# Graph attention over edges: accumulation moved to TensorE and ScalarE

## The reference

```python
q, k, v = x @ Wq + bq, x @ Wk + bk, x @ Wv + bv      # by node, 8 heads
logits = einsum('ehd,ehd->eh', q[dst], k[src]) / sqrt(D)
seg_max = segment_max(logits, dst)
expv = exp(logits - seg_max[dst])
denom = segment_sum(expv, dst)
agg = segment_sum(expv / denom[dst] * v[src], dst)
out = agg + x @ Wskip + bskip                        # then gelu, residual, layer norm
```

## Time and profile before

| | us |
|---|---|
| median of 3 runs | 4432.44 (4432.07 to 4436.84) |
| the profiled execution | 4432.26, its span 4430.5 |
| VectorE busy | 3621.0 (82%) |
| TensorE busy: matmul, weight load | 3266.7 (74%), 2350.0 (53%) |
| GpSimd busy | 2724.9 (62%) |
| ScalarE busy | 2404.3 (54%) |

### The profile page before, as it was taken

One profiled execution on the slowest core, in us unless ns is written; L12 is line 12 of the kernel. 1 busy time (PEld: TensorE's weight loads), 2 busy tenths in 40 slices (PEclk: granted clock), 3 DMA queues, 4 the chain that ended last, 5 costly groups with the idle time before them and its releaser, 6 DMA issues. The chain is left out here.

```text
span 4430.5 us, 103464 instructions
## 1 busy us (share of the span) xinstructions
PE 3266.7 (74%) x25228; PEld 2350.0 (53%) x25229; DVE 3621.0 (82%) x10151; ACT 2404.3 (54%) x5817; POOL 2724.9 (62%) x2719
## 2 busy tenths in 40 slices
PE   7886877877787877878787877347888888887620
PEld 3335666666666666666666666244555555555410
DVE  8888989989898988989898989876666676676457
ACT  4435666666566656666665666454555555555310
POOL 3226766667666766667676665117777777777750
PEclk9988999999999999999999999558999999999855
DMA  6537767667677766777676766521121121111147
GB/s 221 176 124 222 220 207 212 206 208 218 206 212 207 221 203 204 212 208 219 195 221 206 221 200 185 194 95 22 30 34 31 30 34 31 31 30 30 26 83 279
DMA packets 367713, 677.14 MB, mean 153 GB/s; under 512 B 70294, under 2 KB 240482, under 8 KB 367074
## 3 DMA queue, kind: packets, MB, share of 16 engines
q0 software_dynamic: 157888, 420.64, 35.7%
q1 hardware_dynamic: 97474, 128.43, 8.3%
q10 hardware_dynamic: 111712, 120.75, 8.1%
HBM read 582.00 MB, written 87.58 MB: 151 GB/s over the span
## 5 line engine op out<-in xcount | busy, mean ns | idle before, releaser
L736 POOL DMA_INDIRECT KV<-kv_d,src_i x1564 | 1609.1, 1029 | 798.6 <-issue 438.1
L1370 POOL DMA_INDIRECT re_src<-src_tab_d,rsrc x1024 | 985.0, 962 | 311.9 <-issue 245.2
L997 PE MATMUL agg_ps<-msg,oh 128*128 128x264 f32 x3512 | 872.2, 392 | 12.7 <-DVE msg L827 12.7
L997 PEld LDWEIGHTS agg_ps<-msg,oh 128*128 128x128 f32 x3512 | 639.3, 192 | 130.2 <-issue 34.1
L956 PE MATMUL Q<-q,ohT 128*128 128x256 bf16 x5328 | 672.7, 277 | 1.7 <-issue 0.5
L827 DVE TENSOR_TENSOR msg<-KV,msg 128x1024 f32<-128x1024 f32 x439 | 538.4, 1226 | 154.9 <-issue 107.8
L885 ACT ACTIVATE off<-dst_f,wbase 128x4 f32 x447 | 132.9, 297 | 854.7 <-issue 806.6
L893 ACT ACTIVATE square<-iota_b,off 128x128 bf16<-128x128 bf16 x1784 | 568.1, 389 | 0.3
L835 DVE TENSOR_TENSOR prod<-KV,Q 128x1024 f32<-128x1024 f32 x443 | 538.0, 1214 | 3.3 <-issue 1.3
L839 DVE TENSOR_REDUCE lg<-prod 128x32 f32<-128x1024 f32 x443 | 535.5, 1209 | 0.2
L956 PEld LDWEIGHTS Q<-q,ohT 128*128 128x128 bf16 x5328 | 496.3, 99 | 64.1 <-issue 2.2
(11 more groups left out here) (259 smaller groups left out, 5618.6 us busy)
## 6 DMA issues: line engine op xcount, KB each, us to landing
q<-q_d ACTq DMA_DIRECT2D x446, 192.0 KB
y_d<-ex_y ACTq DMA_DIRECT2D x56, 448.0 KB
rg_ye<-y_d SPq DMA_DIRECT2D x7, 3584.0 KB, 12.0
KV<-kv_d,src_i POOLq DMA_INDIRECT x1564
nu_xs<-xs_d SPq DMA_DIRECT2D x7, 2688.0 KB, 11.8
re_src<-src_tab_d,rsrc POOLq DMA_INDIRECT x1024
kv_d<-pr_kv SPq DMA_DIRECT2D x49, 256.0 KB, 2.2
xs_d<-pr_xs SPq DMA_DIRECT2D x49, 256.0 KB, 2.3
```

Source lines behind the costliest of these rows:

```text
L736: pool.indirect_dma_start(out=KV[:, t % (KVR * G), :], out_offset=None, in_=k.kv_d, in_offset=bass.IndirectOffsetOnAxis(ap=k.src_i[:, t:t ...
L997: m = pe.matmul(agg_ps[:, 0:HEADS * HW], oh32[ring(s, 2)][:, t, :], msg[ring(s, 2)][:, t, :, :].rearrange("p h e -> p (h e)"), start=(t == ...
L1370: pool.indirect_dma_start(out=gs[:, t % (RING * RG), :], out_offset=None, in_=k.src_tab_d, in_offset=bass.IndirectOffsetOnAxis(ap=k.rsrc[: ...
```

## The change

On VectorE, `difference`, `add_sums` and `keep_max` go. The logit less its reference is made in PSUM on TensorE: a product of the logits with a negated identity (`minus`), on which the references are accumulated; ScalarE's exponential reads the result with the opposite sign. `scale_sums` writes to a tile of its own, `scaled`, which TensorE adds to the sums by a product with the identity. ScalarE puts the total back into `k.acc` (`keep_sums`) and keeps the maxima (`keep_max`). The references move to the bank of the sums, and `references`, `sums` and `weights` get waits for it. ScalarE's `fetch` goes to SyncE, which runs it in the loop, and SyncE's two waits for the ring go to GpSimd, which now tells that group n - 1 has landed once it has issued the gathers of group n.

```diff
@@ attend: tiles
-        dl = sb("dl", [P, TG], F32)
+        minus = sb("minus", [P, P], F32)
+        scaled = sb("scaled", [P, HEADS * HW], F32)
...
-        ref_ps, max_ps = node_ps[:, 0, 0:TG], node_ps[:, 1, 0:TG]
+        max_ps = node_ps[:, 0, 0:TG]
         agg_ps = ps("agg_ps", [P, 512], F32)
+        ref_ps = agg_ps[:, 512 - TG:512]
@@ GpSimd
+                def landed(n):
+                    pool.wait_ge(kv_landed[n % 4], 16 * G * (n // 4 + 1))
+                    pool.sem_inc(ok["tiles"], G)
                 for n in range(NG):
-                    if n >= 4:
-                        pool.wait_ge(kv_landed[n % 4], 16 * G * (n // 4))
-                        pool.sem_inc(ok["ring_seen"], 1)
                     if n >= KVR:
-                        pool.wait_ge(ok["used"], n - KVR + 1)
+                        old = n - KVR
+                        end = pool.value_load(k.last_tab[0:1, old:old + 1], min_val=1, max_val=RUN)
+                        pool.wait_ge(ok["msg"], end)
+                        pool.sem_inc(ok["used"], 1)
                     for t in range(n * G, (n + 1) * G):
                         pool.indirect_dma_start(...)
+                    if n:
+                        landed(n - 1)
+                landed(NG - 1)
@@ SyncE: the loop over groups goes; fetch comes over from ScalarE, unchanged but for the engine
+                def body(s, last):
+                    if there(s + 7):
+                        fetch(s + 7)
+                walk(sp, body, 7)
@@ VectorE
-                def difference(s):
-                    v.wait_ge(ok["maxima"], s.v + 2)
-                    v.tensor_tensor(dl[:, :], lg[s.slot][:, :], ref_ps, ALU.subtract).then_inc(ok["dl"], 1)
-                def keep_max(s):
-                    v.wait_ge(ok["m_fall"], s.v + 1)
-                    v.tensor_scalar(node_max(s), m_new[:, :], 1.0, None, ALU.mult).then_inc(ok["m_all"], 1)
                 def scale_sums(s):
                     v.wait_ge(ok["fac"], s.v + 1)
                     v.wait_ge(ok["acc"], s.v + 1)
-                    v.tensor_tensor(sums(s), sums(s), bc(fac...), ALU.mult).then_inc(ok["scaled"], 1)
+                    v.tensor_tensor(scaled[...], sums(s), bc(fac...), ALU.mult).then_inc(ok["scaled"], 1)
-                def add_sums(s):
-                    v.wait_ge(ok["agg"], s.v + 1)
-                    v.wait_ge(ok["scaled"], s.v + 1)
-                    v.tensor_tensor(sums(s), sums(s), agg_ps[...], ALU.add).then_inc(ok["acc"], 1)
...
+                v.tensor_scalar(minus[:, :], k.ident[:, :], -1.0, None, ALU.mult).then_inc(ok["cleared"], 1)
@@ ScalarE
+                def keep_sums(s):
+                    w = window(s)
+                    act.wait_ge(ok["agg"], s.v + 1)
+                    act.copy(k.acc[:, bass.ds(w, 1), :]..., agg_ps[:, 0:HEADS * HW]).then_inc(ok["acc"], 1)
                 def weights(s):
-                    act.wait_ge(ok["dl"], s.v + 1)
-                    act.activation(msg[...], dl[...], ACT.Exp, scale=SCALE).then_inc(ok["p"], 1)
+                    act.wait_ge(ok["maxima"], s.v + 2)
+                    if there(s + (-1)):
+                        act.wait_ge(ok["agg"], s.v)
+                    act.activation(msg[...], ref_ps..., ACT.Exp, scale=-SCALE).then_inc(ok["p"], 1)
+                def keep_max(s):
+                    act.copy(k.m_all[:, bass.ds(window(s), 1), :]..., m_new[:, :]).then_inc(ok["m_all"], 1)
                 def body(s, last):
                     if there(s + (-1)):
                         weights(s + (-1))
+                    if there(s + (-2)):
+                        keep_sums(s + (-2))
                     if there(s + (-1)):
                         wide(s + (-1))
                     if there(s + 7):
                         one_hot(s + 7)
                     if there(s):
                         act.wait_ge(ok["m_fall"], s.v + 1)
                         act.activation(fac[...], m_fall[...], ACT.Exp, scale=SCALE).then_inc(ok["fac"], 1)
+                        keep_max(s)
                     if there(s + 6):
                         turn_copy(s + 6)
-                    if there(s + 7):
-                        fetch(s + 7)
                     offsets(s + 8)
+                    if there(s) and not last:
+                        window(s + 1)
@@ TensorE
                 def references(s):
                     pe.wait_ge(ok["m_new"], s.v + 1)
+                    if there(s + (-1)):
+                        pe.wait_ge(ok["p"], s.v)
+                    if there(s + (-2)):
+                        pe.wait_ge(ok["acc"], s.v)
+                    pe.matmul(ref_ps, minus[:, :], lg[s.slot][:, :], start=True, stop=False)
                     for t in range(G):
-                        pe.matmul(ref_ps[...], ohT[...][:, t, :], m_new[:, :], start=True, stop=True)
+                        pe.matmul(ref_ps[...], ohT[...][:, t, :], m_new[:, :], start=False, stop=(t == G - 1))
                 def sums(s):
                     pe.wait_ge(ok["oh32"], s.v + 1)
                     pe.wait_ge(ok["msg"], s.v + 1)
+                    pe.wait_ge(ok["acc"], s.v + 1)
                     for t in range(G):
...
+                    pe.wait_ge(ok["scaled"], s.v + 1)
+                    pe.matmul(agg_ps[:, 0:HEADS * HW], k.ident[:, :], scaled[:, :], start=False, stop=True).then_inc(ok["agg"], 1)
```

More of the change, by code:

```diff
@@ L738, in _, with fetch @@
                                                 ).then_inc(kv_landed[n % 4], 16)
+                    if n:
+                        landed(n - 1)
+                landed(NG - 1)
             @block.sync
             def _(sp):
[L742 to L749, removed]
+                def fetch(s):
+                    w = load(sp, k.w_tab, s, NW - 1)
+                    if there(s + (-LOOP)):
+                        sp.wait_ge(ok["running"], s.v - (LOOP - 1))
+                        sp.sem_inc(ok["resets_seen"], 1)
+                    sp.dma_start(q3[s.slot][:, :], k.q3_d[bass.ds(w * P, P), :]).then_inc(window_landed[s.slot], 16)
+                    g = load(sp, k.g_tab, s, NT - G)
+                    sp.dma_start(reset[s.slot][:, :], k.reset_d[bass.ds(g, G), :, :].rearrange("t h p -> (t h) p")
+                                 ).then_inc(window_landed[s.slot], 16)
+                def body(s, last):
+                    if there(s + 7):
+                        fetch(s + 7)
+                walk(sp, body, 7)
                 for i, s in enumerate(window_landed):
@@ L816, in scale_sums @@
                     v.wait_ge(ok["acc"], s.v + 1)
-                    v.tensor_tensor(sums(s), sums(s), bc(fac[ring(s, 2)][:, :].unsqueeze(2), [P, HEADS, HW]), ALU.mult).then_inc(ok["scaled"], 1)
-                def add_sums(s):
-                    v.wait_ge(ok["agg"], s.v + 1)
-                    v.wait_ge(ok["scaled"], s.v + 1)
-                    v.tensor_tensor(sums(s), sums(s), agg_ps[:, 0:HEADS * HW].rearrange("p (h e) -> p h e", e=HW), ALU.add).then_inc(ok["acc"], 1)
+                    v.tensor_tensor(scaled[:, :].rearrange("p (h e) -> p h e", e=HW), sums(s), bc(fac[ring(s, 2)][:, :].unsqueeze(2), [P, HEADS, HW]), ALU.mult).then_inc(ok["scaled"], 1)
                 def message(s):
@@ L864, in body @@
                     logits(s + 4)
-                    if there(s):
-                        keep_max(s)
                     if there(s) and not last:
@@ L870, in _, with window @@
                 v.memset(k.acc[:, :, :], 0.0).then_inc(ok["acc"], 1)
+                v.tensor_scalar(minus[:, :], k.ident[:, :], -1.0, None, ALU.mult).then_inc(ok["cleared"], 1)
                 v.memset(k.m_all[:, :, :], -BIG).then_inc(ok["cleared"], 1)
-                v.wait_ge(ok["cleared"], 1)
+                v.wait_ge(ok["cleared"], 2)
                 walk(v, body, 4, enter)
                 enter()
-                difference(LAST)
-                add_sums(LAST + (-1))
                 message(LAST)
                 scale_sums(LAST)
-                add_sums(LAST)
             @block.scalar
             def _(act):
+                windows = {}
+                def window(s):
+                    if s.offset not in windows:
+                        windows[s.offset] = load(act, k.w_tab, s, NW - 1)
+                    return windows[s.offset]
+                def keep_sums(s):
+                    w = window(s)
+                    act.wait_ge(ok["agg"], s.v + 1)
+                    act.copy(k.acc[:, bass.ds(w, 1), :].rearrange("p a f -> p (a f)"), agg_ps[:, 0:HEADS * HW]).then_inc(ok["acc"], 1)
                 def offsets(s):
@@ L896, in one_hot @@
                     act.activation(oh[ring(s, OHR)][:, :, :], square[:, :, :], ACT.Relu, bias=k.one[:, :], scale=-1.0).then_inc(ok["oh"], 1)
[L898 to L906, removed]
                 def turn_copy(s):
@@ L912, in weights @@
                 def weights(s):
-                    act.wait_ge(ok["dl"], s.v + 1)
```

(9 more changed lines are left out.)

18 lines of the change are left out of this document (8 added, 10 removed).

## The result

The changed kernel takes 4357.4 us (4355.8 to 4362.6) against 4434.6 us before, a ratio of 0.983 with an interval of 0.981 to 0.984. That is 77 us less, where 58 were forecast; 4374 was the forecast time and 4318 to 4458 its range.

What follows compares the result with a forecast made beforehand. VectorE's list with its register load was taken as the bound, 5.11 us per step, with the ring close behind. Steps of 5.14 instead of 5.28 us, over 415, save 58 us: 4432 - 58 = 4374 us, range 4318 to 4458.

Steps and rivals of the forecast that it cites:

- What bounds the kernel before: VectorE's instructions, 5.28 us per step in the mean, and the message's wait for a register load and its address arithmetic.
- add_sums: On VectorE ahead of the message: of its 0.60 us, removal gives back only one issue place, 0.09 us.
- The long step in four: VectorE's longer wait ahead of the message in one step of four stays: 0.36 us, 0.09 in the mean.
- The difference: On VectorE between tile maxima and message: within the stretch whose shortening, add_sums included, was taken as 0.09 us.
- The ring: Round of waits from references over sums, exponentials and ScalarE's copy back to the references: 4.93 to 5.08 us.
- Which of the two binds: Per step, VectorE at 5.11 us stands over the ring's 4.93 to 5.08; each sometimes waits for the other.
- The sign that the prediction named for being wrong there: On VectorE, the message waits for the exponentials rather than for issue; no size given.
- The sum of 5.14 us: Step length taken from VectorE's 5.11 and the ring's 4.93 to 5.08, since each sometimes waits for the other.
- The steps outside: Loop turns left at their price; the gain counted on 415 ordinary steps, 5.28 to 5.14 us, 58 us.
- The negated identity: Made once, at a cost under 1 us.
- The queues: SyncE's loads, 2.1 us per step, and GpSimd's added waits and register load are hidden.
- The sentence on the bank: By the skill's PSUM rule the ring can't be loosened while references share the sums' bank; without it, VectorE's 5.11 us alone.

Runs made afterwards that it cites:

- e1: The kernel before with the queue moves alone (ScalarE's fetch to SyncE, SyncE's two waits to GpSimd): 4430.3 us, ratio 0.999.
- e7: e1 with VectorE's register load of the window number moved from ahead of the message to behind the product: 4377.4 us, ratio to the kernel before 0.987.
- e2: The changed kernel with difference and keep_max left on VectorE and the references in the maxima's bank: 4354.3 us, ratio to the kernel before 0.982.
- e3: The changed kernel with the references in the maxima's bank and the waits changed, so the ring is open: 4313.6 us, ratio to the kernel before 0.973.
- e8: The changed kernel with VectorE's register load moved from ahead of the message to behind the product: 4355.0 us, ratio to the kernel before 0.982.
- e5: The changed kernel with the negated identity made by ScalarE ahead of its walk, not by VectorE: 4348.2 us, ratio to the kernel before 0.980.
- e10: The changed kernel with VectorE's negated identity issued only once both memsets are done: 4346.7 us, ratio to the kernel before 0.980.
- e6: e3 with VectorE's register load moved from ahead of the message to behind the product: 4252.7 us, ratio to the kernel before 0.959.

## Why the prediction was right, and where it was not

The time came out within 17 us, but three terms were off and one bound was named wrongly. That the time came out is in part luck: VectorE was put too long and the ring too short, and the two are close enough for the sum to land on the right step.

- **What bounds the kernel before.** Right: VectorE's list and the register load ahead of the message. e1 shows that ScalarE wasn't a bound, e7 that the load was.
- **add_sums.** Right in the ordinary step: of its 0.60 us the step gets one issue place back, 0.09 forecast, 0.11 measured in the median (e2). The wait for issue grew to 0.44 (e2) and 0.54 us (e3), where the ring is open; in the changed kernel itself the wait for the exponentials stands there.
- **The long step in four.** Mis-sized. Its 0.36 us, 0.09 in the mean, were kept in the sum. Without add_sums the mean's excess over the median shrank from 0.11 (e1) to 0.04 (e2) and 0.03 (e3: mean 5.07, median 5.04). VectorE alone needs 5.07 us, not 5.11. The delay was a late start of the register load, in 94 of 398 steps, and in none without add_sums; what made it late stays open.
- **The difference.** Taking it off VectorE gave its step nothing: from the tile maxima to the message it is 1.18 us in the median of e2, with it, and 1.18 in e3, without. Of the second half of the change only keep_max counts there, 0.07 us as forecast (5.11 to 5.04).
- **The ring.** Right as a mechanism, with 4.93 to 5.08 forecast and 5.13 measured in the round shown, 5.12 in the median. One part was mis-sized: from the references to the queries 0.34 forecast, 0.48 measured in that round and in the mean, 0.45 in the median. The rest agrees: identity 0.61 of 0.61, exponentials 0.11 of 0.12, copy 0.38 of 0.41, handovers 0.09 and 0.15 within 0 to 0.15 and 0.15, negated identity 0.22 of 0.21. In e3, where nothing waits for the copy, the stretch from the maxima's first product to the queries is 0.23 again, as before, so the 0.14 us (0.38 in the round shown, 0.34 in the median) belong to the closed ring; what of it they are stays open.
- **Which of the two binds.** Wrong. VectorE was put at 5.11 and the ring below it; it is the other way, 5.12 to 5.14 (e8) over 5.07 (e3). The sign that the prediction named for being wrong there, a message that waits for the exponentials rather than for issue, is what the waits show: 246 us against 50. The sum of 5.14 us came out right (5.15 in the mean) since both were close, and not because the right one was taken.
- **The steps outside.** 5.31 less 5.15 in the mean of the ordinary steps is 0.17 us, 69 us for 415 of them; 58 were forecast, from the 5.28 of four steps. The turns of the loop with the steps behind them, left at their price, gave 0.65 us each, 8 us in all, and the head of the walk lost 9. That makes all but some 2 of the 70 us between the two profiled executions. The medians are 77 us apart, as the profiled execution of the changed kernel was 5 us over its median and that of the kernel before 2 us under.
- **The negated identity.** Mis-sized. "Under 1 us" was 0.16 us of VectorE, but by the held gather 9 to 11 us of the kernel (e5, e10).
- **The queues.** Right: hidden, 4430.3 (e1), with no gain that can be told. GpSimd has slack in the changed kernel, 284 us of waiting for the message, and none in e6.
- **The sentence on the bank.** The rule of the Trainium skill that two engines must be kept apart by semaphores per bank (PSUM — Partial Sum Buffer, section "PSUM bank collisions raise a hardware error") is what the ring's waits are there for, and the changed trace agrees that they cost the step: the ring's 5.13 us, over the 5.07 of e3. The rule forbids the overlap, not the choice of the bank; e3 shows what the choice is worth, 44 us. With the maxima's bank the same care costs the exponentials a wait for the tile maxima, and they still end 0.68 us ahead of the message in e3; with the load moved (e6) only 0.15 us are left.

By parts the 77 us are: queues 4, accumulation 76, difference and maxima on TensorE and ScalarE minus 3; the 4 and the 3 are no more than what such a comparison can't tell from nothing. The second half of the change gave nothing as it was placed. With the references in the other bank it is worth 41 us (e2 to e3).

## What to carry to other kernels

An instruction that covers a register load may be worth its own time only after the load is moved: look for "issue" ahead of the instruction behind it, and move the load first, since that is one line. When work is moved to idle engines, walk every closed round of waits that it makes (here sums, exponentials, copy, references) and compare its length with the step, and not only the busy times. Two results that share a PSUM bank tie their readers and writers together, so pick the neighbour whose reader is early. And when the first bound goes, look for the next ones: here TensorE and GpSimd stood 0.1 to 0.3 us behind.

## What the runs showed of the hardware

A gather of GpSimd is held by some instructions of VectorE. From the kernel before, the message on VectorE and two gathers:

```profile
2002.89 1.23 DVE L827 TENSOR_TENSOR msg<-KV,msg 128x1024 f32<-128x1024 f32 x1 [0.20 <-issue]
```

```profile
2002.99 1.95 POOL L736 DMA_INDIRECT KV<-kv_d,src_i  x1 [0.30 <-issue]
2005.24 0.95 POOL L736 DMA_INDIRECT KV<-kv_d,src_i  x1 [0.30 <-issue]
```

The gather that starts 0.10 us into the message takes 1.95 us and ends after it, the next takes 0.95. Over the kernel before, gathers that start in a message's first 0.2 us take 1.76 us in the mean (57 of them), and those that start outside of messages 0.95, also under the product. The message takes 1.23 us whether a gather is under way at its start or not, so only the gather is seen to wait. The message reads two tiles in SBUF, the product one there and one in PSUM. That fits a rule of the Trainium skill (SBUF — State Buffer, section "Who interferes with whom"): a VectorE instruction with two SBUF inputs contends with a GpSimd instruction that reads SBUF, and the one that comes second is fully blocked. The traces agree with it in these numbers, for a gather that comes second, but not for every such instruction: `scale_sums` reads two tiles in SBUF as well, and in the kernel before the 109 gathers that start under it take 0.95 us (in e7, where 250 start under it, 1.20). Nor do they agree with the remark in the same list that such an instruction did not stall descriptor writing. It had a price in e6, where the gathers' mean rose from 986 ns in e3 to 1119 ns because 285 of them started in the first 0.6 us of a message, against 35. A single instruction queued behind a memset held one gather for 12.8 us (e5, e10); whether by the same lock is not shown.
